# Graph layers in 32 groups: another order of work, other PSUM places and another split between engines in the drain

## The reference

```python
h = x @ W_loop.T;  g = h @ Wg_loop.T
vals = (h + b_loop) * sigmoid(g + bg_loop)
x1 = layernorm(x + relu(adj_t @ vals))
y = (adj @ x1) @ weight[0] + bias
out = layernorm(x1 + y)
```

## Time and profile before

| | |
|---|---|
| median of 3 runs | 169.39 us (169.31 to 169.51) |
| the profiled execution: its time | 168.68 us |
| its span | 166.9 us |
| PE busy | 151.6 us, 91% |
| DVE busy | 146.7 us, 88% |
| ACT busy | 126.0 us, 75% |
| POOL busy | 78.6 us, 47% |

### The profile page before, as it was taken

The page is one execution under the profiler, slowest core; times in us unless marked ns, Lnnn a source line. Parts: engine busy times, 40 slices in busy tenths (PEclk is TensorE's granted clock), DMA queues, the critical chain, the costliest instruction groups (busy, mean ns, idle before and its releaser), DMA issues.

```text
span 166.9 us, 3913 instructions
## 1 busy us (share of the span) xinstructions
PE 151.6 (91%) x1072; PEld 140.4 (84%) x1072; DVE 146.7 (88%) x583; ACT 126.0 (75%) x287; POOL 78.6 (47%) x192
## 2 busy tenths in 40 slices
PE   6864899999999999999999999999999999998920
PEld 2553689999999999999999999999999999997910
DVE  1225999999999999999999999999999999999771
ACT  3266455679888888888888889998888888844661
POOL 2700366155555555565555555555554544446000
PEclk9999999999999999999999999999999999999985
DMA  4999999965999999999999899999995341131133
GB/s 137 342 389 394 397 401 403 308 196 189 298 302 306 310 304 274 280 312 301 268 305 329 272 277 333 325 310 298 253 324 212 85 166 63 65 130 63 64 125 138
DMA packets 19465, 42.76 MB, mean 256 GB/s; under 512 B 2160, under 2 KB 3056, under 8 KB 19440
## 3 DMA queue, kind: packets, MB, share of 16 engines
q1 hardware_dynamic: 13968, 25.24, 44.0%
q0 software_dynamic: 4608, 16.78, 33.2%
q10 hardware_dynamic: 864, 0.46, 0.9%
HBM read 34.08 MB, written 8.39 MB: 254 GB/s over the span
## 4 chain that ended last, share of the span: by engine, by line
PE 78%; DMA 8%; DVE 7%; issue 3%; ACT 1%; ACTq 0%; DVEq 0%
PE hg_ps L379 28%; PE msg_ps L409 16%; PE y_ps L430 15%; PE loop_ps L391 15%; DMA b<-msg_bias_dram 5%; DMA gate_b<-gate_bias_dram 2%; PE hg_ps L430 2%; PE hg_ps L426 2%; DVE s_sb L735 2%; DVE stats L742 1%; PE y_ps L426 1%; PE hg_ps L409 1%; ACT out_sb L551 1%; DVE z_sb L753 0%; DVE tiny L679 0%
## 5 line engine op out<-in xcount | busy, mean ns | idle before, releaser
L379 PE MATMUL hg_ps<-w_gate,xt_sb 128*128 128x256 f32 x256 | 60.8, 380 | 2.6 <-ACT hg_ps L515 2.5
L328 POOL TENSOR_SCALAR x<-s_sb,rstd,nmr 128x128 f32<-128x128 f32 x125 | 54.7, 446 | 3.7 <-DVE rstd L691 0.4
L379 PEld LDWEIGHTS hg_ps<-w_gate,xt_sb 128*128 128x128 f32 x256 | 46.2, 190 | 8.5 <-issue 3.0
L320 POOL TENSOR_TENSOR nmr<-mean_neg,rstd 128x4 f32<-128x4 f32 x31 | 6.0, 194 | 68.8 <-DVE rstd L691 68.8
L551 ACT ACTIVATE out_sb<-z_sb,rstd 128x128 f32<-128x128 f32 x112 | 38.0, 391 | 0.2 <-DVE rstd L691 0.2
L391 PEld LDWEIGHTS loop_ps<-vals,adj_sb 128*128 128x128 f32 x256 | 33.3, 191 | 5.2 <-issue 3.8
L391 PE MATMUL loop_ps<-vals,adj_sb 128*128 128x128 f32 x256 | 34.0, 276 | 2.6 <-DVE s_sb L735 2.6
L524 ACT ACTIVATE gate<-hg_ps 128x512 f32<-128x512 f32 x32 | 19.1, 597 | 22.2 <-PE hg_ps L379 22.1
L515 ACT ACTIVATE hg_ps<-gate_b 128x1024 f32<-128x1024 f32 (+1 forms) x32 | 32.3, 1010 | 1.0 <-DMA gate_b<-gate_bias_dram 1.0
L409 PE MATMUL msg_ps<-adjt_sb,x 128*128 128x128 f32 x248 | 33.0, 276 | 0.0
L430 PE MATMUL y_ps<-w,msg_t 128*128 128x128 f32 x232 | 30.6, 275 | 0.0
(11 more groups left out here) (66 smaller groups left out, 104.9 us busy)
## 6 DMA issues: line engine op xcount, KB each, us to landing
xt_sb<-x_t_dram SPq DMA_DIRECT2D x32, 256.0 KB, 4.9
x_sb<-x_dram SPq DMA_DIRECT2D x32, 256.0 KB, 5.0
adj_sb<-adj_dram POOLq DMA_DIRECT2D x16, 512.0 KB, 5.5
adjt_sb<-adj_t_dram POOLq DMA_DIRECT2D x16, 512.0 KB, 5.2
out<-out_sb SPq DMA_DIRECT2D x32, 256.0 KB, 4.1
gate_b<-gate_bias_dram ACTq DMA_DIRECT2D x1, 128.0 KB, 3.4
w_loop<-w_loop_dram ACTq DMA_DIRECT2D x1, 64.0 KB, 2.0
wg_t<-wg_loop_t_dram SPq DMA_DIRECT2D x1, 64.0 KB, 2.2
```

Source lines behind the costliest of these rows:

```text
L328: last = nc.gpsimd.tensor_scalar(x1[:, q % X1_RING, batch(b)], s_sb[:, q % S_RING, batch(b)], r[:, b:b + 1], n[:, b:b + 1], ALU.mult, ALU.add)
L379: last = nc.tensor.matmul(hg_ps[:, q % 2, b, :], xt_sb[:, q % XT_RING, batch(b)], w_gate[:, :], start=False, stop=True, skip_group_check=True)
```

## The change

The loop over the steps stays. What follows it is written anew:

- `LAST` is 27 in place of 28, so five groups are treated as last ones. They have two chains: `CHAIN_A` for 27, 28, 29 (12 columns) and `CHAIN_B` for 30, 31.
- PE adds x1 through the identity for 28, 29 and 31 (`INJECTED`); for 27 and 30 DVE does it (`last_second_sum`). The y of 28, 29, 30, 31 are in banks 0 to 3, the messages of 30 in `loop_ps`.
- The x1 of groups 29, 30 and 31 (`SHARED`) is made in halves: graphs 2 and 3 on ACT (`shared_norm1`), 0 and 1 on POOL, for 31 on DVE.
- The last two ordinary chains of DVE are woven into each other, and into `first_sum` and `first_stats` of group 31.
- `norm2` of group 27 is on POOL (`last_norm2`, new there), of 28, 29 and three graphs of 30 on ACT, the fourth of 30 on POOL, of 31 on DVE.
- SP stores 28, 27, 29, 31 in this order; ACT's own queue stores 30.
- `x1` has 5 places in place of 4. The ring of `out_sb` stays at 4.

```diff
-LAST = GROUPS - 4
+LAST = GROUPS - 5
+CHAIN_A, CHAIN_B = (LAST, LAST + 1, LAST + 2), (LAST + 3, LAST + 4)
+INJECTED = (GROUPS - 4, GROUPS - 3, GROUPS - 1)
+SHARED = (GROUPS - 3, GROUPS - 2, GROUPS - 1)
...
-        msg_place = {GROUPS - 2: bank[3]}
-        y_place = {GROUPS - 3: bank[0], GROUPS - 2: bank[1], GROUPS - 1: bank[2]}
+        msg_place = {GROUPS - 2: loop_ps[:, :]}
+        y_place = {GROUPS - 4: bank[0], GROUPS - 3: bank[1], GROUPS - 2: bank[2], GROUPS - 1: bank[3]}
...
+            sp.wait_ge(out_done, LAST + 1)
+            store(LAST + 1)
+            sp.wait_ge(out_pool, 1)
+            store(LAST)
+            sp.wait_ge(out_done, LAST + 2)
+            store(LAST + 2)
+            sp.wait_ge(out_dve, 1)
+            store(LAST + 4)
...
-                    for b in range(GB) if q < GROUPS - 1 else (2,):
-                        last = nc.gpsimd.tensor_scalar(
+                    for b in range(2 if q in SHARED else GB):
+                        done = nc.gpsimd.tensor_scalar(
...
+            def last_norm2(q, graphs):
+                pool.wait_ge(last_done[q in CHAIN_B], CHAIN_OPS)
+                pool.wait_ge(out_st[q % OUT_RING], 16 * (q // OUT_RING))
+                for b in graphs:
+                    c = (q - LAST) * GB + b
+                    done = nc.gpsimd.tensor_scalar(out_sb[:, q % OUT_RING, batch(b)], z_sb[:, q % Z_RING, batch(b)],
+                                                   last_rstd[:, c:c + 1], zero[:, 0:1], ALU.mult, ALU.add)
+                done.then_inc(out_pool, 1)
...
+            last_norm2(LAST, range(GB))
+            last_norm2(LAST + 3, (3,))
...
+            inject(GROUPS - 4)
+            messages(GROUPS - 3)
             message_weights(GROUPS - 4)
-            messages(GROUPS - 3)
+            inject(GROUPS - 3)
+            messages(GROUPS - 2)
             message_weights(GROUPS - 3)
-            messages(GROUPS - 2)
+            messages(GROUPS - 1)
             message_weights(GROUPS - 2)
...
-            messages(GROUPS - 1)
+            inject(GROUPS - 1)
             message_weights(GROUPS - 1)
...
+            def shared_norm1(q):
...
+                for b in (2, 3):
+                    last = nc.scalar.activation(x1[:, q % X1_RING, batch(b)], s_sb[:, q % S_RING, batch(b)],
+                                                ACT.Identity, bias=nmr[:, t % 2, b:b + 1],
+                                                scale=rstd[:, t % RSTD_RING, 0, b:b + 1])
+                last.then_inc(x1_act, 1)
...
             copy_messages(GROUPS - 4)
-            norm2(GROUPS - 7, every)
+            shared_norm1(GROUPS - 3)
+            norm2(LAST - 2, every)
             copy_messages(GROUPS - 3)
-            norm2(GROUPS - 6, every)
+            shared_norm1(GROUPS - 2)
+            shared_norm1(GROUPS - 1)
+            norm2(LAST - 1, every)
             copy_messages(GROUPS - 2)
...
-            norm2(GROUPS - 5, every)
             copy_messages(GROUPS - 1)
-            norm2(GROUPS - 4, every)
-            norm2(GROUPS - 3, every)
-            norm2(GROUPS - 2, every)
+            norm2(LAST + 1, every)
+            norm2(LAST + 2, every)
+            norm2(LAST + 3, (0, 1, 2))
+            act.wait_ge(out_done, LAST + 3)
+            act.wait_ge(out_pool, 2)
+            act.dma_start(out[LAST + 3], out_sb[:, (LAST + 3) % OUT_RING, :])\
+                .then_inc(out_st[(LAST + 3) % OUT_RING], 16)
...
+            def last_second_sum(q):
...
+                tt(z_sb[:, q % Z_RING, :], y_of(q), x1[:, q % X1_RING, :], ALU.add).then_inc(last_z, 1)
...
             def last_norm2(q):
-                dve.wait_ge(last_done[(q - LAST) // 2], CHAIN_OPS)
-
-                await_count(dve, out_st[q % OUT_RING], 16 * (q // OUT_RING))
+                dve.wait_ge(last_done[q in CHAIN_B], CHAIN_OPS)
+
+                dve.wait_ge(out_st[q % OUT_RING], 16 * (q // OUT_RING))
...
-            for t in range(GROUPS + 1):
+            for t in range(GROUPS):
...
+            steps, last_steps, odd_steps = chain(LAST_CHAIN - 1), chain(LAST_CHAIN), find_odd()
+            next(steps)
+            next(steps)
+            next(steps)
+            first_sum(GROUPS - 1)
+            next(steps)
+            first_stats(GROUPS - 1, 0)
+            next(steps)
+            first_stats(GROUPS - 1, 1)
+            next(steps)
+            for _ in steps:
+                next(last_steps)
+            for _ in last_steps:
+                next(odd_steps, None)
             last_norm1(GROUPS - 1)
...
+            last_second_sum(LAST)
+            for q in CHAIN_A:
+                last_second_stats(q, 0)
+                last_second_stats(q, 1)
+            steps = last_chain(0, CHAIN_A)
+            for _ in range(6):
                 next(steps)
+            last_second_sum(LAST + 3)
+            next(steps)
+            last_second_stats(LAST + 3, 0)
+            next(steps)
+            last_second_stats(LAST + 3, 1)
+            next(steps, None)
```

More of the change, by code:

```diff
@@ L252, in store @@
             def store(q):
[L253 to L258, removed]
+                sp.dma_start(out[q], out_sb[:, q % OUT_RING, :]).then_inc(out_st[q % OUT_RING], 16)
             sp.dma_start(wg_t[:, :], wg_loop_t).then_inc(fold_in, 16)
@@ L269, in _ @@
             load_x(3)
-            for t in range(GROUPS + NORM2_LAG):
+            for t in range(LAST + NORM2_LAG):
                 load_xt(t + 5)
                 load_x(t + 4)
-                store(t - NORM2_LAG)
+                if 0 <= t - NORM2_LAG < LAST:
+                    sp.wait_ge(out_done, t - NORM2_LAG + 1)
+                    store(t - NORM2_LAG)
+            sp.wait_ge(out_done, LAST + 1)
[6 more added lines that the diff above has]
+            store(LAST + 4)
             def general_loads():
@@ L339, in _ @@
             load_adjt(1)
-            for t in range(GROUPS + NORM1_LAG):
+            pool.wait_ge(table_ready, 2)
+            for t in range(GROUPS + NORM1_LAG - 1):
                 norm1(t - NORM1_LAG)
@@ L411, in messages, with inject @@
                     last.then_inc(msg_done, 1)
+            def inject(q):
+                pe.wait_ge(ident_in, 16)
+                pe.wait_ge(vals_done, GROUPS - 1 if q < GROUPS - 2 else GROUPS)
+                if q < GROUPS - 1:
+                    pe.wait_ge(x1_done, q + 1)
+                else:
+                    pe.wait_ge(x1_dve, 1)
+                if q in SHARED:
+                    pe.wait_ge(x1_act, q - SHARED[0] + 1)
+                for b in range(GB):
+                    nc.tensor.matmul(y_of(q)[:, batch(b)], ident[:, :], x1[:, q % X1_RING, batch(b)],
+                                     start=b == 0, stop=False, skip_group_check=True)
             def message_weights(q):
@@ L418, in message_weights @@
                     if q in y_place:
-                        pe.wait_ge(vals_done, GROUPS)
+                        pe.wait_ge(vals_done, GROUPS - 1 if q < GROUPS - 2 else GROUPS)
                     else:
                         await_count(pe, z_done, q)
[L422 to L427, removed]
                     pe.wait_ge(msgt_done, q + 1)
@@ L430, in message_weights @@
                         last = nc.tensor.matmul(y_of(q)[:, batch(b)], msg_t[:, q % 2, batch(b)], w1[:, :],
-                                                start=q < LAST, stop=True, skip_group_check=q >= LAST)
+                                                start=q not in INJECTED, stop=True,
+                                                skip_group_check=q in INJECTED)
                     last.then_inc(y_done, 1)
@@ L541, in norm2 @@
                     else:
-                        act.wait_ge(last_done[(q - LAST) // 2], CHAIN_OPS)
+                        act.wait_ge(last_done[q in CHAIN_B], CHAIN_OPS)
                     await_count(act, out_st[q % OUT_RING], 16 * (q // OUT_RING))
                     for b in graphs:
[L546 to L551, removed]
+                        c = (q - LAST) * GB + b
+                        r = rstd[:, t % RSTD_RING, 1, b:b + 1] if q < LAST else last_rstd[:, c:c + 1]
+                        z = y_of(q) if q in INJECTED else z_sb[:, q % Z_RING, :]
+                        last = nc.scalar.activation(out_sb[:, q % OUT_RING, batch(b)], z[:, batch(b)], ACT.Copy,
+                                                    scale=r)
                     if graphs[-1] >= 2:
                         last.then_inc(out_done, 1)
+            def shared_norm1(q):
+                t = q + NORM1_LAG
+                if q < GROUPS - 1:
+                    act.wait_ge(nmr_done, q + 1)
+                else:
+                    act.wait_ge(last_nmr, 1)
+                act.wait_ge(msg_done, q - X1_RING + 1)
+                act.wait_ge(z_done, q - X1_RING + 1)
+                for b in (2, 3):
[3 more added lines that the diff above has]
+                last.then_inc(x1_act, 1)
             def look(q):
@@ L710, in negative_means, with last_chain @@
```

(8 more changed lines are left out.)

101 lines of the change are left out of this document (46 added, 55 removed).

## The result

| | before | changed |
|---|---|---|
| median of 12 runs | 169.45 us (169.04 to 170.16) | 170.05 us (169.61 to 170.57) |
| the profiled execution, its span | 166.9 us | 168.4 us |
| ratio to before, 95% interval | | 1.0033 [1.0019, 1.0048] |

A forecast was written before the change was run, and what follows sets the result against it. The drain, from about 147 us, was taken to decide: 1.5 us won on DVE, 2.0 of waiting for a store, 0.4 saved at the end. Span 166.6, 0.3 less than 166.9, so 169.39 - 0.3 = 169.1 us; range 168.2 to 170.4.

The forecast's parts named there:

- DVE's new order: DVE in the drain: first_sum of group 31 starts 1.59 us earlier, its chain ends 1.74 us earlier, chain A at 157.87.
- Chain B: DVE's last chain, groups 30 and 31: ends at 160.5, so DVE is ready for last_norm2 1.5 us earlier.
- a rival: DVE and POOL hold each other up beside chain B: hidden on DVE's side, 0.5 us on POOL's, 169.6 us; chance 0.08.
- PE and ACT: Drain: y of group 31 is done at 157.6 in place of 159.4, before DVE wants it at 157.87.
- The wait that takes the place: DVE's last_norm2 waits until group 27's store frees its out_sb place: 2.0 us of waiting, which eats the 1.5 won.
- I take 2.7: Landing time in us assumed for group 27's store, from an earlier store of that group; ends 2.0 and 4.1.
- PE's earlier end: PE ends 1.8 us earlier, so the instruction packet may fall before the stores; an argument against the slow landing.
- The rival of the slow landing: Group 27's store is held up by the instruction packet and lands after 4.1 us: 170.5 us; chance 0.25.
- its own bound of 3.4 us: Landing time of group 27's store from which the slow-landing rival decides, the sum then over 0.34 us above the median.
- mine: The prediction's own case: group 27's store lands after between 2.0 and 3.3 us; chance 0.62.
- The saving of 0.4 us at the end: Last store travels alone, ACT issuing group 30's: 0.4 us off the 3.29 from last issue to span's end.
- the slower side: Total time slower than before by more than what can't be told from none (above 169.73 us); chance 0.29.

The follow-up runs named there:

- a_flag_late: The changed kernel, four places, with DVE writing the flag only after its last norm2: 170.06 us, ratio 1.0059 to the kernel before.
- a_pe_late: The changed kernel, four places, with PE waiting for chain B's fifth operation before it reads the flag and branches: 168.60 us, ratio 0.9966 to the kernel before.
- the second profile: Profile of the changed kernel measured once more, nothing altered: 170.06 us, ratio 1.0066 to the kernel before.
- a_r5_pe2_sp30: Changed kernel, five out_sb places, PE waiting for chain B's second operation, group 30 stored by SP, not ACT: 168.01 us, ratio 0.9935 to the kernel before.

## Why the prediction was right in its mechanism and wrong in its sign

- **DVE's new order: right.** With 0.77 us taken off, `first_sum` of group 31 started at 147.67 (147.68 was worked out), the chains ended at 149.99 and 151.46 (149.96, 151.56), chain A at 157.90 (157.87). (Chain A's start adds up to 155.19 from its own terms, not 155.16; measured were 155.06. It moves nothing.)
- **Chain B: half a microsecond long.** 160.5 was worked out, 160.96 measured; its first three operations took 0.24, 0.39 and 0.38 us beside POOL (0.17 each in a quiet stretch). I had put this into a rival and out of the sum. It was hidden under the wait, as that rival said.
- **PE and ACT: right.** The message weights of 31 ended at 158.37 - 0.77 = 157.6, and DVE never waited for them.
- **The wait that takes the place: right in place and cause, too small in size.** POOL was done at 159.73 against 159.80. The failing step is "I take 2.7": the landing took 3.1 us in the first profile and 3.5 in the second. I had the row that says so, the packet of the earlier trace rows and the 4.1 beside it, and had written that the store now goes into this very stretch, but priced it by the store of the same group, which had left 3 us earlier. Even that 2.7 was not an undisturbed landing: a q8 packet of 1.3 us began at 156.66 in the profile before, just as that store was issued. PE's earlier end, which I counted against the slow landing, doesn't take the packet away. The flag is written only 0.8 us sooner than before (157.96 after the 0.77, against 158.76), and the packet came 1.0 to 1.1 us sooner (159.75 and 159.90 against 160.88), right onto the stores. The runs with the packet moved (a_flag_late, a_pe_late) have 2.0 us here. The rival of the slow landing, to which I had given 0.25, was this mechanism; by its own bound of 3.4 us the second profile is its case and the first still mine.
- **The saving of 0.4 us at the end: wrong.** I took 2.9 us from the last issue to the end; it was 3.5, and 3.2 in the second profile, about the 3.29 of before. So there was no saving, and a_r5_pe2_sp30 shows that the second queue was worth nothing that can be told. In the first profile two q14 packets, 1.3 us of one engine, lay between 165 and 166 us beside the last store, and a second q8 packet, 1.4 us from 163.66, ahead of it. Before, two q14 packets of 1.1 us together lay beside the last store too, which landed after 2.8 us; so why it took 3.1 now stays open.
- Together these are 0.4 + 0.6 = 1.0 us, the distance between the 166.6 of my sum and the 167.6 of the profile (0.8 + 0.3 in the second profile); the medians lie 170.05 - 169.1 = 0.95 apart. The time fell inside the range, but on the slower side, to which I had given 0.29.

```profile
q14 instruction: 2, 0.02, 8.0%
```

That window, 165 to 166 us of the changed kernel's first profile, shows the packets beside the last store.

## What to carry to other kernels

When work is moved so that something new waits for a buffer to be stored and freed, look at what else uses the DMA engines in that very stretch, and price the landing by a store of that stretch, not by its median. An idle engine's way to its branch is not free: holding it back by one wait moved the changed kernel from +0.66% to -0.34%. And before an operation in a drain gets faster, follow its buffer's ring one lap back: a fifth place took between 0.5% and 0.9% off the changed kernel (1.0033 and 1.0066 against 0.9978, in other sets), where the store one lap back had become late, and nothing off the kernel before, where it hadn't.

## What was not expected of the hardware

- An instruction packet on q8 delays stores. With no instruction packet near them, stores of 256 KB landed after 2.0 to 2.4 us (a_flag_late, all six); with a q8 packet near them, which takes 1.0 to 1.8 us of one of the 16 engines, most took 2.7 to 4.7, and the stores issued shortly before and after it shared the delay. That the one engine is then behind for all of them is the likely reason; no view shows a single engine. The Trainium skill (DMA: Bandwidth & Descriptors, on why a DMA increments its semaphore by 16) says that a store is done only when every engine is; these runs agree, with 4.1 us before and 3.1 and 3.5 now where one engine was taken, and 2.0 where it wasn't.
- The q8 packet followed PE: it moved with the moment from which PE could read the flag and branch. In the eight profiles without PE's wait it began 1.8 to 2.1 us after the flag was written, in the six with it 2.1 to 2.8 us after the operation that PE waited for. That it is PE's own fetch of instructions is inferred from this. When each further packet comes, and why the kernel before has one at 156.66 us that the changed one lacks (with PE's wait it is still there, at 156.94), was not tried and stays open.
- The end of the program has a way of its own: from the flag to the span's end passed 5.1 us in a_flag_late, although the last store had landed 3.1 us before the end.
- DVE's small operations beside POOL's 128x128 instructions took up to 0.40 us in place of 0.17; when POOL had two of four, chain B was 0.45 us shorter.
